# Reordering the prologue of the first attention in a two-layer transformer kernel

## What is computed

```
c_q, c_kv = x @ Wq_down, x @ Wkv_down                 # 512 -> 64
q_c = (c_q @ Wq_up).reshape(b, s, 128, 4)
q_r = (x @ Wq_rope).reshape(b, s, 128, 64)
k_c = (c_kv @ Wk_up).reshape(b, s, 128, 4)
v_c = (c_kv @ Wv_up).reshape(b, s, 128, 4)
k_r = x @ Wk_rope                                     # one for all heads
scores = (q_c . k_c + q_r . k_r) / sqrt(68)
out = softmax(scores) @ v_c ; return out @ Wo
```

## Time and profile before

| | us |
|---|---|
| median of three runs | 2560.16 |
| the profiled execution's own time | 2563.6 |
| its span | 2561.8 |
| first product of the prologue | 5.39 |
| first maximum of row 0 starts | 38.57 |
| first scores of row 0 start | 73.35 |
| row 1 takes over (p0 of the steady order) | 90.63 |
| last product of the first attention starts | 1393.04 |

### The profile page before, as it was taken

One profiled execution on the slowest core, in us unless ns is written; L12 is line 12 of the kernel. 1 busy time (PEld: TensorE's weight loads), 2 busy tenths in 40 slices (PEclk: granted clock), 3 DMA queues, 4 the chain that ended last, 5 costly groups with the idle time before them and its releaser, 6 DMA issues. The chain is left out here.

```text
span 2561.8 us, 40544 instructions
## 1 busy us (share of the span) xinstructions
PE 2479.7 (97%) x12630; PEld 1865.5 (73%) x12630; DVE 1560.0 (61%) x2779; ACT 1391.2 (54%) x2147; POOL 1146.3 (45%) x1146
## 2 busy tenths in 40 slices
PE   8999999999999999999998899899999999999997
PEld 3677777777777777777774588777877877878774
DVE  6566666666666666666663522375756657557556
ACT  3677777777777777777775332232423424324231
POOL 3456555555555565555553233243434335234210
PEclk8899999999999999999998999999999999999998
DMA  6222222222222222222222222111001010010001
GB/s 202 50 44 52 47 53 50 46 52 47 57 44 52 46 53 48 49 52 46 58 44 78 89 87 87 70 38 42 16 25 41 0 41 16 25 41 16 1 1 53
DMA packets 47613, 125.40 MB, mean 49 GB/s; under 512 B 6034, under 2 KB 23442, under 8 KB 41427
## 3 DMA queue, kind: packets, MB, share of 16 engines
q1 hardware_dynamic: 47570, 124.85, 18.2%
HBM read 80.27 MB, written 10.49 MB: 35 GB/s over the span
## 5 line engine op out<-in xcount | busy, mean ns | idle before, releaser
L440 DVE TENSOR_REDUCE row_max<-ps_max 128x1 f32<-128x512 f32 x1024 | 670.7, 687 | 192.4 <-PE ps_max L529 170.6
L294 POOL TENSOR_TENSOR p_parts<-probs,p_parts 128x1024 f16<-128x1024 f32 x256 | 547.7, 2149 | 360.7 <-ACT p_parts L361 360.4
L356 ACT ACTIVATE probs<-ps_score 128x1024 f32<-128x1024 f32 x512 | 523.2, 1022 | 240.8 <-PE ps_score L545 219.8
L543 PE MATMUL ps_score<-Q,K 128*128 128x512 f32 x1024 | 407.8, 398 | 1.6 <-ACT probs L356 1.6
L545 PE MATMUL ps_score<-Q,K 97*128 97x512 f32 x1024 | 407.4, 398 | 0.0
L529 PE MATMUL ps_max<-KX,Q 68*128 68x512 f32 x1024 | 379.5, 412 | 5.0 <-DMA Q<-content_q 1.8
L434 DVE TENSOR_TENSOR Q<-ps_x,Q 64x512 fp32r<-64x512 f32 x254 | 175.2, 690 | 252.9 <-ACT Q L351 249.2
L361 ACT ACTIVATE p_parts<-probs 128x1024 f16<-128x1024 f32 x256 | 269.4, 1052 | 4.0
L529 PEld LDWEIGHTS ps_max<-KX,Q 68*128 68x128 f32 x1024 | 189.2, 190 | 81.1 <-issue 35.2
L543 PEld LDWEIGHTS ps_score<-Q,K 128*128 128x128 f32 x1024 | 194.4, 190 | 59.5 <-ACT probs L356 13.4
L1328 POOL CAST q_hi<-roped 128x512 fp32r<-128x512 f32 x64 | 39.1, 610 | 415.5 <-DVE roped L1448 198.9
(11 more groups left out here) (262 smaller groups left out, 4441.7 us busy)
## 6 DMA issues: line engine op xcount, KB each, us to landing
Q<-Q SPq DMA_DIRECT2D x64, 512.0 KB, 4.3
ffn_raw<-in_w_ffn SPq DMA_DIRECT2D x22, 768.0 KB, 4.4
w_raw<-in_w_qrope SPq DMA_DIRECT2D x32, 512.0 KB, 3.6
wq_raw<-in_wq SPq DMA_DIRECT2D x8, 1024.0 KB, 5.6
wo_raw<-in_wo SPq DMA_DIRECT2D x8, 1024.0 KB, 4.8
content_k<-probs SPq DMA_DIRECT2D x8, 512.0 KB, 5.8
Q<-content_q SPq DMA_DIRECT2D x64, 64.0 KB
K<-content_k SPq DMA_DIRECT2D x64, 64.0 KB
```

Of the source, the lines that this page charges most:

```text
L294: pool.tensor_tensor(p_lo[:, j, :, :], probs[:, j, 0:PAIRED, :], p_hi[:, j, :, :], ALU.subtract)\
L356: act.activation(probs[:, j, 2 * half:2 * half + 2, :], ps_score[half][:, :, :], ACT.Exp, scale=SCALE).then_inc(exped, 1)
L440: dve.tensor_reduce(row_max[:, t, j:j + 1], ps_max[t % 2][:, :], axis=AXX, op=ALU.max)\
L543: pe.matmul(ps_score[half][:, k, :], K1[:, b, t * P:(t + 1) * P], Q1[:, b, j, :], start=True, stop=False)
```

## The change

It moves work within the prologue and row 0, on five engines.

On PE, each pair of maxima of row 0 is followed by exactly one filler: a product of job r of sequence 1 for the first four pairs, a third of the first queries of row 1 for the next three, and the first value tile for the last. The other seven value tiles stand behind T. Row 0 of the loop's order leaves out its steps p, whose products have been issued by then. The waits for the last job and for the spread rope keys move from the first maximum of row 1 to the first scores of row 0. Value tiles now turn over three banks instead of four.

On DVE, all zeros and the row of ones are written by memsets at the start (L464 becomes six of them), and POOL's copies for these go. The rope keys of sequence 1 (`rope_keys(1)`) stand behind all maxima instead of between the two halves of them. On ACT the high part of the first query weights stands behind nine jobs, and seven copies of value tiles behind `mrow`. On SP only block 0 is stored ahead of the content rows, and block 1 behind them.

```
@@ bank
-            k = n % 8 if n < N_R else n % 4
+            k = n % 8 if n < N_R else n - N_R + 2 if n < N_V else (n - N_V) % 3
@@ SP
             store(0)
-            store(1)
             sp.wait_ge(parts_out[0], 64)
-            sp.wait_ge(zeros_set, 2)
-            sp.wait_ge(rows_set, 4)
+            sp.wait_ge(zeros_set, 4)
             for b in range(NB):
                 max_keys(0, b)
                 content(0, b)
-            store(2)
-            store(3)
+            for m in range(1, DC):
+                store(m)
@@ POOL
-            pool.memset(zeros[:, :], 0.0).then_inc(set_up, 1)
...
-            for tile in (Q2, K2):
-                pool.tensor_copy(tile[ROPE:P, 1, :, :], zeros[ROPE:P, :].rearrange("p (a s) -> p a s", a=1)
-                                 .broadcast_to([ROPE, GH, S])).then_inc(rows_set, 1)
...
-            for b in range(NB):
-                pool.tensor_copy(K2[MROW:MROW + 1, b, :, :], ones[MROW:MROW + 1, :].rearrange("p (a s) -> p a s", a=1)
-                                 .broadcast_to([1, GH, S])).then_inc(rows_set, 1)
@@ ACT
-            act.wait_ge(w_in, 16)
-            for pair in range(2):
-                act.activation(w_hi[:, :, pair, :], w_raw[:, :, pair, :], ACT.Copy).then_inc(w_step, 1)
...
-            for n in range(N_R):
+            for n in range(N_R // 2):
                 job(n)
-            job(N_R)
+            act.wait_ge(w_in, 16)
+            for pair in range(2):
+                act.activation(w_hi[:, :, pair, :], w_raw[:, :, pair, :], ACT.Copy).then_inc(w_step, 1)
+            for n in range(N_R // 2, N_R + 1):
+                job(n)
             high(0, 0, 0)
             high(0, 0, 1, ps_o)
             job(N_R + 1)
-            for n in range(N_V, N_V + 6):
-                job(n)
-            act.wait_ge(job_made, len(jobs))
-            for n in range(N_V + 6, len(jobs)):
-                job(n)
+            job(N_V)
...
                         if kind == "A" and more:
                             high(n + 1, 1 - b, 0)
+                        if kind == "A" and not before:
+                            for t in range(1, TT):
+                                if t == 6:
+                                    act.wait_ge(job_made, len(jobs))
+                                job(N_V + t)
@@ DVE
-            dve.wait_ge(set_up, 1)
-            for tile in (Q2, K2):
-                dve.tensor_copy(tile[ROPE:P, 0, :, :], zeros[ROPE:P, :].rearrange("p (a s) -> p a s", a=1)
-                                .broadcast_to([ROPE, GH, S])).then_inc(zeros_set, 1)
+            for b in range(NB):
+                for tile in (Q2, K2):
+                    dve.memset(tile[ROPE:P, b, :, :].bitcast(F32), 0.0).then_inc(zeros_set, 1)
+            dve.wait_ge(zeros_set, 2 * NB)
+            for b in range(NB):
+                dve.memset(K2[MROW:MROW + 1, b, :, :].bitcast(F32), 1.0).then_inc(zeros_set, 1)
...
-                if pair == 0:
-                    rope_keys(1)
+            rope_keys(1)
@@ PE
-            first_max(0)
-            first_max(1)
-            job(N_R + 1, (0,))
...
-            for t in range(TT):
-                if t < 5:
-                    first_max(6 + 2 * t)
-                    first_max(7 + 2 * t)
-                job(N_V + t)
-            pe.wait_ge(set_up, 8)
+            for pair in range(2 * GH):
+                first_max(2 * pair)
+                first_max(2 * pair + 1)
+                if pair < DC:
+                    job(N_R + 1, (pair,))
+                elif pair < DC + 3:
+                    queries(0, 1, 0, pair - DC)
+                else:
+                    job(N_V)
+            pe.wait_ge(set_up, 6)
...
-                        if kind == "p" and more:
+                        if kind == "p" and more and before:
...
+                        if kind == "T" and not before:
+                            for v in range(1, TT):
+                                job(N_V + v)
+                            pe.wait_ge(rope_set, NB * GH)
+                        if kind == "s" and not before and at == [0, 0]:
+                            pe.wait_ge(job_high, len(jobs))
+                            pe.wait_ge(rope_low, NB)
+                        if kind == "s" and first and at == [0, 0]:
+                            pe.wait_ge(rope_spread, b + 1)
...
-                        if first and b == 0 and (kind, at) == ("m", [0, 0]):
-                            pe.wait_ge(job_high, len(jobs))
-                            pe.wait_ge(rope_set, NB * GH)
-                            pe.wait_ge(rope_spread, NB)
```

More of the change, by code:

```diff
@@ L108, in mla_stage @@
         zeros_set = sem("zeros_set")
-        rows_set = sem("rows_set")
         rope_set = sem("rope_set")
@@ L140, in mla_stage @@
         w_krope = V[:, 4, :].rearrange("p (c n) -> p c n", c=DC)
-        ones = V[:, 3, :]
-        zeros = oT
         def step_list(text):
@@ L310, in body @@
                         low_p(n, j)
-            pool.memset(zeros[:, :], 0.0).then_inc(set_up, 1)
-            pool.wait_ge(set_up, 1)
-            pool.memset(ones[MROW:MROW + 1, :], 1.0).then_inc(set_up, 1)
-            pool.wait_ge(set_up, 2)
             for slot in (V_slot, V_parts):
                 pool.memset(slot[:, :, :, :, :], 0.0).then_inc(set_up, 1)
-            pool.wait_ge(set_up, 4)
+            pool.wait_ge(set_up, 2)
             for slot in (V_slot, V_parts):
@@ L321, in _ @@
             pool.memset(ident[:, :], 0.0).then_inc(set_up, 1)
-            pool.wait_ge(set_up, 7)
+            pool.wait_ge(set_up, 5)
             pool.affine_select(out=ident[:, :], in_=ident[:, :], compare_op=ALU.not_equal, fill=1.0,
                                base=0, pattern=[[-1, P]], channel_multiplier=1).then_inc(set_up, 1)
-            pool.wait_ge(set_up, 8)
-            for tile in (Q2, K2):
-                pool.tensor_copy(tile[ROPE:P, 1, :, :], zeros[ROPE:P, :].rearrange("p (a s) -> p a s", a=1)
-                                 .broadcast_to([ROPE, GH, S])).then_inc(rows_set, 1)
-            pool.wait_ge(rows_set, 2)
-            pool.wait_ge(zeros_set, 2)
-            for b in range(NB):
-                pool.tensor_copy(K2[MROW:MROW + 1, b, :, :], ones[MROW:MROW + 1, :].rearrange("p (a s) -> p a s", a=1)
-                                 .broadcast_to([1, GH, S])).then_inc(rows_set, 1)
-            pool.wait_ge(rows_set, 4)
+            pool.wait_ge(set_up, 6)
             for pair in range(2):
@@ L572, in turn_o, with job @@
                 last.then_inc(o_turned, 1)
-            def job(n, parts=(0, 1)):
+            def job(n, chunks=range(DC)):
                 kind, m, b = jobs[n]
-                if parts[0] == 0 and n >= 8:
-                    before = n - 8 if n < N_V else n - 4
+                if chunks[0] == 0 and n >= 8:
+                    before = n - 8 if n < N_V else N_R - 2 + n - N_V if n < N_V + 3 else n - 3
                     pe.wait_ge(job_high, before + 1)
@@ L580, in job @@
                         pe.wait_ge(job_low, before + 1 - NB)
-                    elif N_R <= before < N_V:
-                        pe.wait_ge(rope_low, before - N_R + 1)
+                    elif before == N_R:
+                        pe.wait_ge(rope_low, 1)
                 out = bank(n)
                 if kind == "r":
-                    if parts[0] == 0:
+                    if chunks[0] == 0:
                         pe.wait_ge(krope_in, 16)
-                    for c in range(2 * parts[0], 2 * parts[-1] + 2):
+                    for c in chunks:
                         last = pe.matmul(out, w_krope[:, c, :], xT[:, c, b * S:(b + 1) * S], start=c == 0, stop=c == DC - 1)
-                    if parts[-1] == 0:
+                    if chunks[-1] != DC - 1:
                         return
@@ L624, in first_max @@
                 max_scores(0, 0, 0, k // 4, k % 4, wait_free=k >= 2)
-            first_max(0)
-            first_max(1)
-            job(N_R + 1, (0,))
-            first_max(2)
-            first_max(3)
-            job(N_R + 1, (1,))
-            first_max(4)
-            first_max(5)
-            for t in range(TT):
-                if t < 5:
-                    first_max(6 + 2 * t)
-                    first_max(7 + 2 * t)
-                job(N_V + t)
-            pe.wait_ge(set_up, 8)
+            for pair in range(2 * GH):
[8 more added lines that the diff above has]
+            pe.wait_ge(set_up, 6)
             def body(g, first, last):
```

## The result

| | median us (range, executions) | ratio to before [95%] |
|---|---|---|
| before | 2557.84 (2555.37 to 2563.22, 13) | |
| changed | 2552.95 (2548.79 to 2556.59, 13) | 0.9978 [0.997, 0.9987] |

The change makes the kernel faster by 0.22%, some 5 us; the forecast was 2550, in a range of 2542 to 2557. The profiled execution of the changed kernel took 2552.97 (span 2551.1), its median to 0.02 us. That of before took 2563.6, 5.8 above the median of its 13. Against the one trace that it started from, the forecast was 2553.5, and the profiled execution came within 0.6 us of that; against the medians the gain is half of the 10.1 us that the sum gave. The median lies in the range all the same. The rest of this text is about that half.

A forecast was written before the change was run, and what follows sets the result against it. PE, busy 97%, bounds the kernel; the gain arises in the prologue ahead of s01. Steps 3 to 6 sum to -10.1 us, 2563.6 profiled to 2553.5, with the median 3.4 below: 2550, range 2542 to 2557.

The forecast's parts named there:

- Step 1: DVE's front: six memsets of 2.1 replace two copies, the split of x runs quiet; low parts at 21.6, +0.3 us.
- Rival B: DVE's front: memsets as fast as the cast, -4.3 us there, 2545.5 in all; chance 8%.
- Rival E: DVE's front: the split of x stays slow without POOL, +8 us, 2558, no change; chance 5%.
- Step 2: PE among the jobs: resumes near 15.4, then idles 3.2 us for DVE's first low part; +0.8, between 0 and +3.1.
- Step 3: First maximum: PE's 1.76 us wait for the content rows goes, start at 37.9 instead of 38.57; -0.7 us.
- Step 4: Row 0's eight pairs of maxima: full clock, 12.6 us instead of 18.4, last pair at 50.5; -5.8 us.
- Step 5: From the last pair of maxima to the first scores: 14.1 us instead of 16.4, first scores at 64.6; -2.3 us.
- Step 6: From row 0's first scores to its second score group s01: 7.0 us instead of 8.32; -1.3 us.
- Rival A: Value tiles keep full clock: 6.3 us instead of 10.8, 6.6 less with the scores behind, 2543.5; chance 20%.
- Rival D: Idle among the jobs drops PE's clock at 22.3 and it stays down: s01 at 93.7, +12 us, 2572; chance 5%.

The follow-up runs named there:

- the front alone: The kernel before with only the six DVE memsets, POOL's copies gone and ACT's query weights' high part behind nine jobs: 2558.11 us, ratio 0.9996.
- the experiment without the pause: The changed kernel with DVE's second low part of the queries, and its wait for block 1's stores, behind all 16 maxima: 2554.55 us, 0.9985 to before.

## Why the prediction was right and wrong

**Step 1** came out: memsets of 2.1, low parts at 21.31 (21.6). Rival B would need low parts near 17. The Trainium skill (VectorE: DVE Perf Modes, section on zero memsets issued as uint32) gives one cycle per element, and the starts 2.14 apart agree (the prediction has 2.13 by it). The step's own bounds are off by a little: six memsets of 1.4 or 2.3 instead of 2.1 give -3.9 and +1.5, not -4.3 and +1.3. Rival E did not occur: the split was quiet. It depends on what POOL does: with memsets there the casts took 1.11 and the subtractions still 1.23, against 2.79 beside POOL's copies. That these two were short only while POOL did not copy is not quite so: the subtraction of 1.23 at 6.01 ran on beside POOL's first copy, which began at 6.19.

**Step 2** had the idle (3.51, said 3.2) but too small a price. The clock fell at once, to 0.50, and was back at full only near 29, at the end of the jobs: PE was free for the first maximum at 38.70, not 37.9. In the second trace of the changed kernel the clock fell 2 us later and for 3.4 us, and PE was free at 37.68. The total does not show the cost (the front alone).

**Step 3** was right in its mechanism (no DMA wait), and its start late by the 0.8 of Step 2.

**Step 4** failed in one term: "Block 1's stores, now issued from 34 on, take 5.2 to 7 and land by 42; DVE needs them at 44.7". They had landed by 45.15 and 45.46 only in the two traces of the changed kernel, at 294 to 364 GB/s for the first 4.5 us. DVE was there before, waited 0.42 and 1.76, and PE stood for 1.11 and 2.45. The first time the clock stayed, the second time it fell, for 27 us. The last pair of the first trace (50.57, said 50.5) agrees by luck: the step began 0.8 late, and its spacings came to 11.87 instead of 12.6, the pause of 1.11 included. In the experiment without the pause they came to 10.41.

**Step 5** failed in its cover: "`mrow`'s wait for all stores ends near 51, ahead of T". It ended at 55.73, 3.3 behind T. I had divided 6.3 MB by 400 GB/s; the rate was below that both in the first slices from 34.6 on and in the last, from 50.8 on (264, 218, 127, 100). The bound behind it failed as well: "`mrow` can be 8 us late before the tiles stop hiding it" counted PE's tiles alone. Their copies are queued behind `mrow` on ACT and there are three banks, so PE stops after three more tiles, whatever it has left to do. T at 52.45 (said 52.5), first scores at 65.02 (64.6) and the mark at 72.15 (71.6) agree to 0.6, but the tiles' share is another: three at full clock, 2.25 of idle and four in 5.77 (at half clock from 59.3 on), instead of two at 0.9 and five at 1.8. Both add up to 10.8 from the first of the seven to the last: right total by luck, wrong parts.

**Step 6**, 7.0 said, 7.13 measured. Rival A (tiles at full clock) is what the traces show wherever the tiles found a full clock and PE did not stop among them: 6.27 to 6.45, in five of them. Rival D did not occur: the clock was at full again near 29, ahead of job r at 29.66.

**The sum** went by one trace as if the clock's falls belonged to the program. With three traces of before the mark averages 79.0, (81.67 + 79.52 + 75.85) / 3, with two of after 74.9: 4.1 earlier, beside 4.9 of the medians. The forecast took 81.67 alone and said 10.1; with 81.67 and 72.15 it is 9.5. Of the 6 us between 10.1 and 4.1, 2.7 are the excess of the starting trace over the mean of three, and 3.3 are what the two traces of after reach the mark later than 71.6, on average. The sentence "the median of the runs is 3.4 below" took the long prologue off the level and left it in the difference. The mis-sized terms are thus the products at half clock in Steps 4 to 6: from the first maximum to the mark PE was at half clock for 30.7, 27.3 and 20.5 us in the three traces of before, and for 10.2 and 27.3 in the two of after. That the profiled execution came within 0.6 us of 2553.5 is luck, since the second trace of the same kernel reached the mark 5.6 later. Two things stay open. Five traces are few for a mean. And a microsecond at the mark is not always one at the end, as the prediction takes it: from the mark to the end of the span the fourteen traces need 2476 to 2480 us, and the trace that it read is among the longest there too (2480.1).

## What to carry to other kernels

Where PE's clock can fall, a pause of one or two microseconds can cost what runs behind it at half clock, so price each wait by what follows it, and profile a kernel two or three times before a difference of 0.3% is worked out from one trace. A transfer that is moved behind another is late by all that it now stands behind; ask for each waiter which instructions stand in line behind the waiting one, and how many banks their readers leave free. Of two waits in a row the removal of either alone may show nothing: try both together before either is dropped.

## What was not expected of the hardware

- In none of the fourteen traces did the clock rise while value tiles ran, plain float32 products on 64 rows. Seven tiles took 6.27 behind a busy PE at full clock and 12.31 behind one at half clock, both without idle, and PE was at 0.50 from 50 to 70 in the second trace of the changed kernel while busy 20.00 of 20.00, and from 57.02 to 69.26 with the seven tiles alone. They do not keep a full clock for certain: in the first trace of the changed kernel it fell among them, 1.2 us after PE had resumed from a pause of 2.25. The Trainium skill (TensorE: Matmul & The Clock Gate, section What's actually happening) has the clock follow the array's activity; why these products leave a low clock low, though PE is never idle in them, no run here shows.
- In the changed kernel and its variants, idle of 0.72 and 1.11 us in the maxima left the clock at full; idle of 2.45 to 3.50 in the same place, in five traces, was each time followed by half clock. But the length of the pause does not decide it alone. In the order of before, with value tiles among the maxima, the clock fell behind idle of 0.76, and in the third trace of before at 46.2, where PE had been busy for 2.5 us since idle of 0.56:

```profile
43.70 1.10 PE L529 MATMUL ps_max<-KX,Q 68*128 68x512 f32 x2 [0.56 <-DVE row_max L440]
...
46.57 2.07 PE L598 MATMUL ps_score<-w_up,V 64*128 64x512 f32 x2
```

- Among the jobs, idle of 2.81 and 2.50 left it at full, while 2.29 in the second trace of before was followed by half clock at once. What decides, there and in the maxima, is open.
- A DVE memset of 2048 elements is shown as 1.76 and occupies 2.14, by the starts. The busy times of the page are too small for it by the difference.
- Memsets on POOL slow DVE's casts beside them (0.69 to 1.11, the first one 1.33 and 1.78) and leave two-operand subtractions at 1.23; POOL's own went from 1.80 to 2.34.
